# Projection of the next head pair emitted between the attention units of this one, with score tiles of two key blocks

## What is computed

```python
Q = circulant(x, wq_c, wq_b); K = circulant(x, wk_c, wk_b); V = circulant(x, wv_c, wv_b)
attn_logits = einsum('bqhd,bkhd->bhqk', Q, K) * 64 ** -0.5      # 16 heads of 64
attn_weights = softmax(attn_logits, axis=-1)
out = circulant(einsum('bhqk,bkhd->bqhd', attn_weights, V), wo_c, wo_b)
```

## Time and profile before

| | us |
|---|---|
| median of the timed runs (2) | 5848.33 |
| lowest and highest | 5742.74, 5953.92 |
| the profiled execution | 5747.3 |
| its span on the slowest core | 5745.0 |
| spans of the 8 cores | 5711.0 to 5745.0 |

### The profile page before, as it was taken

How to read it: one execution, slowest core, us unless ns; L and a number is a source line. 1 busy time by engine, 2 the same in 40 slices (tenths; PEclk the granted TensorE clock), 3 DMA queues, 4 the chain that set the end, 5 groups by cost and what they waited for, 6 DMA issues and landing times.

```text
span 5745.0 us, 56438 instructions; the slowest of 8 cores (5711.0 to 5745.0 us)
## 1 busy us (share of the span) xinstructions
PE 4815.2 (84%) x18656; PEld 1758.4 (31%) x18656; DVE 1626.2 (28%) x2454; ACT 1470.5 (26%) x1310; POOL 86.8 (2%) x107
## 2 busy tenths in 40 slices
PE   1788888888888888888854599999999999999996
PEld 1312212131221312112112244444444444344442
DVE  4212012111111112012113433433333333433334
ACT  2242442434444342442432111011011011011010
POOL 0100000000000000000000000000000000000000
PEclk9856556565565656556556799999999999999997
DMA  6200000000000000000021421223212132122113
GB/s 215 36 0 1 6 0 6 0 6 0 0 6 0 6 0 1 0 0 1 0 55 66 72 34 28 34 34 56 34 28 34 28 61 34 28 34 34 28 28 117
DMA packets 100810, 165.65 MB, mean 29 GB/s; under 512 B 28080, under 2 KB 69056, under 8 KB 100544
## 3 DMA queue, kind: packets, MB, share of 16 engines
q0 software_dynamic: 83072, 94.93, 11.3%
q1 hardware_dynamic: 17472, 67.11, 3.4%
HBM read 240.17 MB, written 16.78 MB: 45 GB/s over the span
## 4 chain that ended last, share of the span: by engine, by line
PE 83%; DVE 9%; issue 3%; DMA 2%; ACT 2%; DVEq 0%; POOL 0%; ACTq 0%; SPq 0%; POOLq 0%
PE psGU L77 27%; PE psO L77 22%; PE psS L77 18%; PE psD L77 14%; DVE invl L77 4%; ACT PT L77 2%; PE psT L77 1%; PE psC L77 1%; DMA xst<-xf 1%; DVE lscr L77 1%; DVE stg L77 1%; DMA out<-obuf 1%; DVE us_sb L77 0%; DMA co_sb<-co 0%; DVE xnst L77 0%
## 5 line engine op out<-in xcount | busy, mean ns | idle before, releaser
L77 ACT ACTIVATE PT<-psS,consts 128x1536 bf16<-128x1536 f32 (+1 forms) x704 | 1117.4, 1592 | 1739.0 <-PE psS L77 1739.0
L77 PE MATMUL psO<-PT,Vp 128*65 128x512 bf16 x2048 | 1001.8, 623 | 86.2 <-ACT PT L77 86.2
L77 PE MATMUL psS<-QTp,KTp 64*128 64x512 bf16 x2048 | 952.7, 612 | 4.4 <-DVE Vp L77 4.4
L77 PE MATMUL psD<-prod,wdh 128*128 128x512 bf16 x3520 | 782.8, 379 | 77.6 <-DVE prod L77 76.9
L77 PE MATMUL psGU<-xn2T,wgh 128*128 128x512 bf16 x3520 | 844.1, 383 | 0.0
L77 PE MATMUL psGU<-xn2T,wuh 128*128 128x512 bf16 x3520 | 835.6, 380 | 0.0
L77 ACT ACTIVATE gs_sb<-psGU 128x512 bf16<-128x512 f32 x440 | 262.7, 597 | 2142.8 <-PE psGU L77 2094.5
L77 DVE COPY lscr<-psO 1x512 f32<-1x512 f32 x64 | 41.4, 684 | 1924.4 <-PE psO L77 1924.4
L77 DVE TENSOR_TENSOR yacc<-yacc,psD 128x512 f32<-128x512 f32 x608 | 418.4, 688 | 370.9 <-PE psD L77 370.7
L77 PEld LDWEIGHTS psO<-PT,Vp 128*65 128x65 bf16 x2048 | 243.6, 153 | 817.4 <-issue 816.8
L77 PEld LDWEIGHTS psD<-prod,wdh 128*128 128x128 bf16 x3520 | 321.7, 97 | 538.7 <-issue 243.1
(11 more groups left out here) (105 smaller groups left out, 1261.1 us busy)
## 6 DMA issues: line engine op xcount, KB each, us to landing
xst<-xf SPq DMA_DIRECT2D x16, 2048.0 KB, 9.4
wgh<-wg POOLq DMA_DIRECT2D x8, 1536.0 KB, 15.2
wuh<-wu POOLq DMA_DIRECT2D x8, 1536.0 KB, 24.4
wdh<-wd POOLq DMA_DIRECT2D x8, 1536.0 KB, 31.2
wgh<-wg POOLq DMA_DIRECT2D x8, 1280.0 KB, 13.2
wuh<-wu POOLq DMA_DIRECT2D x8, 1280.0 KB, 20.6
wdh<-wd POOLq DMA_DIRECT2D x8, 1280.0 KB, 25.9
xo<-xf SPq DMA_DIRECT2D x4, 2048.0 KB, 11.3
```

The source lines that it names most:

```text
L77: ins = getattr(e, meth)(*args, **kw)
```

## The change

The attention stage is rebuilt in two ways.

Groups are two key blocks instead of three: 16 groups, 32 units a chunk. `PT` and `psS` shrink to 1024 columns, `psS` to two banks each. The two banks that this frees become `psP`, two tiles for the projection alone.

The projection of pair p+1 is no longer done in front of its attention. A class `ProjQ` holds its 44 jobs. After each unit of pair p, `drain_to` emits as many of them as the share of units done asks for, so PE's order becomes QK(u), PV(u-1), sometimes a job, QK(u+1). The DVE eviction of a job waits for the job and, from p = 1 on, for the last QK and PV of pair p-1, whose buffers it overwrites. The first pair's projection is done at the front as before. Weight transfers are issued two pairs ahead of their attention. Nothing of the tail changes.

```diff
-            PT = cc(nc.sbuf_tensor("PT", [128, 3, 1536], BF16))
+            PT = cc(nc.sbuf_tensor("PT", [128, 3, 1024], BF16))
-            psS = [cc(nc.psum_tensor(f"psS{i}", [128, 1536], F32)) for i in range(2)]
+            psS = [cc(nc.psum_tensor(f"psS{i}", [128, 1024], F32)) for i in range(2)]
             psO = cc(nc.psum_tensor("psO", [128, 1024], F32))
+            psP = [cc(nc.psum_tensor(f"psP{i}", [128, 512], F32)) for i in range(2)]
-            groups = [(3 * g, 3) for g in range(10)] + [(30, 2)]
+            groups = [(2 * g, 2) for g in range(16)]
+            UPC = 32
...
+            class ProjQ:
+                def __init__(self, p, gates):
+                    self.p = p
+                    self.jobs = make_jobs(p)
+                    self.j = 0
+                    self.vp0 = S.n("vP")
+                    self.gates = gates
+                def emit_one(self):
+                    p, kind, idx = self.jobs[self.j]
+                    bp_ = p % 2
+                    pj = psP[self.j % 2][:]
+                    ws = list(wpair_lv[p])
+                    if self.j >= 2:
+                        ws.append(("vP", self.vp0 + self.j - 1))
+                    ev_ws = [("pP", None)] + self.gates
...
+                def drain_to(self, frac):
+                    tgt = min(len(self.jobs), int(len(self.jobs) * frac + 0.999))
+                    while self.j < tgt:
+                        self.emit_one()
...
+            emit_wdma(0)
+            if NPAIR > 1:
+                emit_wdma(1)
+            q0 = ProjQ(0, [])
+            q0.finish()
+
+            for p in range(NPAIR):
+                bp = p % 2
+                if p + 2 < NPAIR:
+                    emit_wdma(p + 2)
+                if p + 1 < NPAIR:
+                    nq = ProjQ(p + 1, [("pQK", pair_end[p - 1]["pQK"]),
+                                       ("pPV", pair_end[p - 1]["pPV"])]
+                               if p > 0 else [])
...
                             if pend is not None:
                                 emit_pv(pend)
                             pend = (u, c, pts, h)
+                            if nq is not None:
+                                nq.drain_to((u + 1) / (NCH * UPC))
```

More of the change, by code:

```diff
@@ L282, in build_program, with emit_wdma @@
             GV = S.n("gc")
-            groups = [(3 * g, 3) for g in range(10)] + [(30, 2)]
+            groups = [(2 * g, 2) for g in range(16)]
+            UPC = 32
             pair_end = {}
-            for p in range(NPAIR):
-                bp = p % 2
-                colsl = slice(128 * p, 128 * (p + 1))
+            proj_pP = {}
+            proj_done = {}
+            wpair_lv = {}
+            def emit_wdma(p):
+                bp_ = p % 2
+                colsl_ = slice(128 * p, 128 * (p + 1))
@@ L291, in build_program @@
                 ws = [("g0a", None), ("g0b", None), ("gc", GV), ("vE", XNT)]
                 if p >= 2:
-                    ws.append(("pP", pair_end[p - 2]["pP"]))
-                for cn, cmat, dst in (("q", cq, cqp[bp]), ("k", ck, ckp[bp]),
-                                      ("v", cv, cvp[bp])):
+                    ws.append(("pP", proj_pP[p - 2]))
+                for cn, cmat, dst in (("q", cq, cqp[bp_]), ("k", ck, ckp[bp_]),
+                                      ("v", cv, cvp[bp_])):
@@ L296, in build_program @@
                     S.op("gpsimd", "dma_start", out=dst[:],
-                         in_=cmat.rearrange("(t p) n -> p t n", p=128)[:, :, colsl],
-                         waits=ws, inc=f"wld{cn}{p % 2}", inck=16)
+                         in_=cmat.rearrange("(t p) n -> p t n", p=128)[:, :, colsl_],
+                         waits=ws, inc=f"wld{cn}{bp_}", inck=16)
                     ws = []
-                WPAIR = [(f"wld{cn}{p % 2}", 16 * (p // 2 + 1))
-                         for cn in ("q", "k", "v")]
@@ L303, in build_program @@
[L303 to L313, removed]
+                wpair_lv[p] = [(f"wld{cn}{bp_}", 16 * (p // 2 + 1))
+                               for cn in ("q", "k", "v")]
@@ new lines, in make_jobs @@
+            def make_jobs(p):
+                return [(p, "q", c) for c in range(NCH)] + \
+                       [(p, "k", kc) for kc in range(NKC)] + \
+                       [(p, "v", kt) for kt in range(32)]
+            class ProjQ:
[7 more added lines that the diff above has]
+                    p, kind, idx = self.jobs[self.j]
+                    bp_ = p % 2
+                    pj = psP[self.j % 2][:]
[3 more added lines that the diff above has]
+                    ev_ws = [("pP", None)] + self.gates
@@ L316, in build_program @@
                             S.op("tensor", "matmul", pj,
-                                 cqp[bp][:, dt, :],
+                                 cqp[bp_][:, dt, :],
                                  xnT[:, dt, idx * 512:(idx + 1) * 512],
@@ L322, in build_program @@
                         S.op("vector", "tensor_scalar",
-                             QTp[bp][:, idx * 512:(idx + 1) * 512], pj,
+                             QTp[bp_][:, idx * 512:(idx + 1) * 512], pj,
                              biasT[:, p:p + 1], None, ALU.add,
-                             waits=[("pP", None)], inc="vP")
+                             waits=ev_ws, inc="vP")
                     elif kind == "k":
@@ L328, in build_program @@
                             S.op("tensor", "matmul", pj,
-                                 ckp[bp][:, dt, :],
+                                 ckp[bp_][:, dt, :],
                                  xnT[:, dt, idx * 512:(idx + 1) * 512],
@@ L334, in build_program @@
                         S.op("vector", "tensor_scalar",
-                             KTp[bp][:, idx * 512:(idx + 1) * 512], pj,
+                             KTp[bp_][:, idx * 512:(idx + 1) * 512], pj,
                              biasT[:, NDT + p:NDT + p + 1], None, ALU.add,
-                             waits=[("pP", None)], inc="vP")
+                             waits=ev_ws, inc="vP")
                     else:
@@ L342, in build_program @@
                                  xnT[:, dt, idx * 128:(idx + 1) * 128],
-                                 cvp[bp][:, dt, :],
+                                 cvp[bp_][:, dt, :],
                                  start=(dt == 0), stop=(dt == NDT - 1),
@@ L346, in build_program @@
                                  inc="pP" if dt == NDT - 1 else None)
-                        dstv = Vp[bp][:, idx, :].rearrange(
+                        dstv = Vp[bp_][:, idx, :].rearrange(
                             "p (a b) -> p a b", b=65)[:, :, 0:64]
@@ L350, in build_program, with finish @@
                         S.op("vector", "tensor_copy", dstv, srcv,
-                             waits=[("pP", None)], inc="vP")
-                PROJ_V = S.n("vP")
-                pair_end[p] = {"pP": S.n("pP")}
+                             waits=ev_ws, inc="vP")
+                    self.j += 1
+                def drain_to(self, frac):
+                    tgt = min(len(self.jobs), int(len(self.jobs) * frac + 0.999))
+                    while self.j < tgt:
+                        self.emit_one()
+                def finish(self):
+                    while self.j < len(self.jobs):
+                        self.emit_one()
+                    proj_pP[self.p] = S.n("pP")
+                    proj_done[self.p] = S.n("vP")
+            emit_wdma(0)
[11 more added lines that the diff above has]
+                               if p > 0 else [])
+                else:
+                    nq = None
                 exp_at = {}
@@ L363, in emit_pv @@
                     ws = [("aE", exp_at[u])]
-                    if u % 22 <= 1:
+                    if u % UPC <= 1:
                         ws.append(("vT", evac_at.get(cc_ - 1, S.n("vT"))
@@ L367, in emit_pv @@
                     vsl = slice(65 * h, 65 * h + 65)
-                    k0_, glen_ = groups[(u % 22) // 2]
+                    k0_, glen_ = groups[(u % UPC) // 2]
                     for i in range(glen_):
@@ L383, in build_program @@
                         for h in range(2):
-                            u = c * 22 + 2 * gi + h
+                            u = c * UPC + 2 * gi + h
                             slot = u % 2
@@ L393, in build_program @@
                                 ws.append(("vT", S.n("vT")))
-                                ws.append(("vP", PROJ_V))
-                            if c > 0 and u == c * 22 + 1:
+                                ws.append(("vP", proj_done[p]))
+                            if c > 0 and u == c * UPC + 1:
                                 ws.append(("vT", recip_at[c - 1]))
@@ L451, in build_program @@
                     evac_at[c] = S.n("vT")
-                pair_end[p]["vT"] = S.n("vT")
+                if nq is not None:
+                    nq.finish()
+                pair_end[p] = {"pQK": S.n("pQK"), "pPV": S.n("pPV"),
+                               "vT": S.n("vT")}
```

(6 more changed lines are left out.)

## The result

| | before | after |
|---|---|---|
| lowest time, us | 5739.70 | 5293.21 |
| median of all runs, us | 5801.86 (10) | 5342.84 (12) |
| profiled span, slowest core, us | 5745.0 | 5292.7 |
| spans of the 8 cores, us | 5711.0 to 5745.0 | 5252.3 to 5292.7 |
| mean granted clock, slowest core | 0.765 | 0.866 |

The ratio of after to before is 0.9245, with a 95% interval of 0.9216 to 0.9273: 7.5% faster.

What follows compares the result with a forecast made beforehand. PE at 1.2 GHz, not ACT, was taken to bound the attention. Its stage, 42 + 7 × 297 + 310 = 2431 us against 2753, gave 5425; 25 more for the slowest core made 5450 us, range 5260 to 5650.

Steps and rivals of the forecast that it cites:

- the forecast as summed: Whole kernel: the summed terms hold, with half the V chunks at the high clock; 5330 to 5530 us, chance 0.50.
- the share of V chunks that find the clock: Chunks 2 and 3 of a pair: half taken to run high, 50 us, half low, 73; mean 62.
- The bound and the clock: Attention stage: PE at 1.2 GHz bounds, not ACT; the share of 128-row work, not busy time, decides the clock.
- Rise behind Q and K jobs: Chunks 0 and 1: clock rises within some 6 us behind Q or K jobs; chunks of 62 and 51 us.
- The unit at the higher clock: Attention units at the higher clock: the loop through ACT takes over; two units take 2.63 us, one 1.32.
- The lower clock's prices: Attention at the lower clock: unit 1.95 us, 32 make 62.4; V job 0.95; V chunk 73 us.
- The tails and boundaries: Ends of chunks and pairs: tail 14.5 us, 0.5 less than now; pair boundary 2 us.
- The 25 us added for the slowest core: Added to 5425, since whether chunks 2 and 3 find the clock differs by core: 5450 us.
- rival D: Chunks 2 and 3: every V chunk is lifted early, 50 us each; pair 273, time 5260 us; chance 0.13.
- B: Attention: clock never rises, QK groups cutting off each job; pair 382, time 6020 us, slower; chance 0.08.
- C: Attention: only Q and K jobs lift the clock, V chunks stay at 73 us; time 5580 us; chance 0.20.
- E: Attention units: clock falls back during exp waits, or loop exceeds 1.32; unit 1.65 us, time 5670; chance 0.09.

## Why the prediction was right, and where it was off

The measured time, 5293 us, lies inside the whole range, 5260 to 5650, but below the 5330 to 5530 of the forecast as summed. The mechanism was right; one term, the share of V chunks that find the clock, was too small.

**The bound and the clock.** Right, and shown: with nothing but the rows of useless matmuls changed, 5664.5 becomes 5048.1 us; with the jobs kept but cut to 64 rows the Q and K chunks stay at 0.50; with the jobs left out the kernel is slower.

**Rise behind Q and K jobs.** Right. Chunk 0 took 62.2 us (mean of 56 over cores and pairs 0 to 6) against 62, chunk 1 49.2 against 51. (The terms for chunk 0 add up to 62.7.) Two of the readings behind it were loose. The 4.9 us to a rise are those of one projection: on that core it came 2.9 to 5.7 us into seven of them, and the first began with the clock up. And the groups at a chunk's end stand in the same order at all 32 ends; what came at 16 of them is the rise. So one and the same pattern found the clock in half the cases there, which is the better ground for taking half in the V chunks.

**The unit at the higher clock.** Right: the loop through two exps gives 1.75 us for units of three key blocks where 1.76 was forecast, and the chunks agree with the 1.32 of units of two.

**The lower clock's prices.** A chunk of V jobs that missed the clock took 72.9 us (forecast 73), one without jobs 64.2 (62.4; the sum left out the wait for the chunk's first exp). A V job at the lower clock, for which no row stood, shows here:

```profile
1504.46 1.06 PE L77 MATMUL psO<-PT,Vp 128*65 128x512 bf16 x2
1505.31 1.06 PE L77 MATMUL psP<-cvp,xnT 128*128 128x128 bf16 x8
1506.30 1.03 PE L77 MATMUL psS<-QTp,KTp 64*128 64x512 bf16 x2
```

PV to QK takes 1.84 us with the job and 1.00 without it, so it adds 0.84 (taken: 0.95, from 0.86 to 1.15).

**The share of V chunks that find the clock: the term that was mis-sized.** "I take half" was a choice. Of the 112 chunks with V jobs alone (chunks 2 and 3 of pairs 0 to 6 on eight cores) 71 took under 52 us, 12 over 70, the rest found it on the way; the mean is 54.5 us against 62. That is 14 × 7.5 = 105 us of the 154 between the sum, 5425, and the mean of the cores, 5271. The tails and boundaries of pairs 0 to 6 were 23 to 29 us shorter in all than charged, chunk 1 gave 12, and the last pair took 5 back. The stage was forecast at 2431 us and took 2293 on the mean of the cores (2314 on the slowest); the last 16 of the 154 us lie outside it. The 25 us added for the slowest core were about right: it lies 22 us over the mean. So the truth lies between the forecast and rival D, near D in time, though not by D's way: there every V chunk was to be lifted early, at 50 us. The 112 chunks are from one execution, and the cores often go in step (in pair 6 all eight took 48.9 to 49.1 us for chunk 2), so 71 of 112 is a count and no general share.

The cause of the spread, that the rise depends on where jobs stand, is shown by the reordered jobs. Why one V chunk catches the clock at its third unit and the next, with the same work, never, I have not shown.

**Rivals.** B, the clock never rises, did not come. The run nearest to its world, the 64-row jobs, is slower than before, as said, but at 5820 us where B had 6020 and the run's own forecast 6060: 64-row work of both halves overlaps, and in 88 chunks the clock rose after all. C and E did not come. The rule of the Trainium skill, TensorE: Matmul & The Clock Gate, Part 1, that activity releases the throttle, holds here only if activity is not read as busy time: 62.5 us with PE busy 61.99 stayed at 0.50.

## What to carry to other kernels

Look at the granted clock beside PE's busy time: a PE that is fully busy at half its clock is not at its limit, and attention with 64-row QK matmuls is such a case. Put work that uses all rows (the next projection, or useless matmuls if there is none) into the waits in which the clock falls and at the start of a stretch that is to run high; in this kernel 38 useless matmuls a chunk were worth 12.9%, more than the careful interleaving. If the same work comes in several orders, choose the one in which every stretch begins with full-row work.

## What the runs showed of the hardware

- The clock of PE rises on work that uses its rows, not on busy time: units at 99% busy stayed at 0.50 for 62.5 us, and 64-row matmuls in all the waits did not lift them, 128-row ones did (5664.5 against 5048.1 us).
- Once up, it stays up on less: 8 matmuls of 64 rows across the wait for the first exp held it at 1.0 for the 39 us of a chunk in which PE was busy 33.95 us, half of it in 64-row matmuls; that came in 64 of 64 first chunks, and in 3 of 64 without the 8.
- Matmuls on rows 0 to 63 and on rows 64 to 127 that stand next to each other overlap: a QK of the second head started with three of the job's eight matmuls still to start, and job and QK together took 3.52 us, where 4.38 went by with a QK on the job's own rows.
